# Attention rounds written out in place of a loop of two rounds, on all five engines of one Trainium2 core

## What is computed

```
x = x + attention(layernorm(x))             # 16 heads of 32, causal, softmax, output projection
x = x + xattn(ctx, ctx, layernorm(x))       # a long convolution of products k*v with a kernel per head, by q
x = x + ffn(layernorm(x))                   # weights and activations rounded to 8 bit, silu(gate) * up, down
```

## Time and profile before

| | us |
|---|---|
| median of 3 runs | 1241.2 (1239.53 to 1241.73) |
| the profiled execution | 1243.32 |
| its span, first to last instruction | 1241.5 |
| start of round 2 to end of round 13 (the loop) | 429.10 |

### The profile page before, as it was taken

How to read it: one execution, slowest core, us unless ns; L and a number is a source line. 1 busy time by engine, 2 the same in 40 slices (tenths; PEclk the granted TensorE clock), 3 DMA queues, 4 the chain that set the end, 5 groups by cost and what they waited for, 6 DMA issues and landing times. The chain is left out here.

```text
span 1241.5 us, 33761 instructions
## 1 busy us (share of the span) xinstructions
PE 1142.1 (92%) x10142; PEld 815.6 (66%) x10142; DVE 1006.6 (81%) x3165; ACT 880.2 (71%) x1815; POOL 963.1 (78%) x1112
## 2 busy tenths in 40 slices
PE   7989999999999999998756799999999999999996
PEld 5767777777777777875435566666666666666652
DVE  4678878878788887887486798888988988988885
ACT  3678888878788887888564366766667666667665
POOL 1286887767777776787833999999999999999993
PEclk8979999999999999999775999999999999999999
DMA  6346755556555555655382444434444333444310
GB/s 206 93 154 193 235 167 171 183 173 190 178 176 171 159 185 166 189 163 182 143 287 70 128 136 142 128 109 131 137 144 140 123 112 129 142 144 132 112 62 26
DMA packets 87840, 186.57 MB, mean 150 GB/s; under 512 B 12176, under 2 KB 28816, under 8 KB 87760
## 3 DMA queue, kind: packets, MB, share of 16 engines
q1 hardware_dynamic: 86896, 185.02, 47.2%
q10 hardware_dynamic: 864, 0.66, 0.3%
HBM read 105.86 MB, written 54.61 MB: 129 GB/s over the span
## 5 line engine op out<-in xcount | busy, mean ns | idle before, releaser
L649 ACT ACTIVATE prob<-masked,negmax 128x128 f32<-128x128 f32 (+1 forms) x512 | 206.4, 454 | 67.6 <-DVE negmax L777 66.6
L777 DVE CUSTOM_DVE_ANT_0 masked<-s_ps,mask_f 128x128 f32<-128x128 f32 (+1 forms) x512 | 161.1, 352 | 34.0 <-PE s_ps L530 21.5
L1028 PE MATMUL y_ps<-kv,toep 128*128 128x288 f16 x640 | 184.2, 288 | 1.4 <-DVE prod L1390 1.4
L1029 PE MATMUL y_ps<-kv,toep 128*128 128x288 f16 x640 | 183.8, 287 | 0.0
L1030 PE MATMUL y_ps<-kv,toep 128*128 128x288 f16 x640 | 183.8, 287 | 0.0
L1086 PE MATMUL f_ps<-w1T,xiT 128*128 128x512 bf16 (+1 forms) x768 | 172.9, 361 | 0.9 <-ACT xiT L1222 0.7
L1286 POOL TENSOR_TENSOR tree<-prod 128x512 f32<-128x512 f32 x128 | 163.3, 1276 | 1.3 <-DVE prod L1390 1.3
L1229 ACT ACTIVATE silu<-gate,sx 128x512 f32<-128x512 f32 (+1 forms) x96 | 66.0, 687 | 134.4 <-DVE gate L1454 134.3
L409 POOL TENSOR_TENSOR kv_s<-kv_f,kv_s 128x1152 f16<-128x1152 f32 x64 | 152.2, 2379 | 0.6 <-ACT kv_s L663 0.6
L783 DVE TENSOR_TENSOR pT_lo<-t_ps,pT_hi 128x384 f16<-128x384 f32 x256 | 140.7, 550 | 12.2 <-ACT pT_hi L657 11.7
L657 ACT CAST pT_hi<-t_ps 128x384 f16<-128x384 f32 x256 | 122.4, 479 | 34.4 <-PE t_ps L539 33.1
(11 more groups left out here) (162 smaller groups left out, 3505.6 us busy)
## 6 DMA issues: line engine op xcount, KB each, us to landing
kv_pairs<-kv_s SPq DMA_DIRECT2D x64, 576.0 KB, 3.3
kv<-kv_pairs SPq DMA_DIRECT2D x32, 1152.0 KB, 8.1
c_in<-in_ctxr SPq DMA_DIRECT2D x64, 192.0 KB, 2.5
x_in<-in_x SPq DMA_DIRECT2D x16, 512.0 KB, 6.4
q_st<-q_hi SPq DMA_DIRECT2D x128, 64.0 KB, 2.0
k_st<-k_hi SPq DMA_DIRECT2D x128, 64.0 KB, 2.0
x_res<-in_x SPq DMA_DIRECT2D x16, 512.0 KB, 5.9
x_after_attention<-x_out SPq DMA_DIRECT2D x16, 512.0 KB, 4.3
```

Of the source, the lines that this page charges most:

```text
L649: ins = nc.scalar.activation(prob[h % 2][:, at:at + w], masked[h % 2][:, at:at + w], ACT.Exp, bias=negmax[:, h % 2, t:t + 1], scale=-1.0)
L777: ins = nc.vector.tensor_tensor_reduce(masked[h % 2][:, at:at + w], s_ps[h % 2][:, at:at + w], mask_f[:, S - w:S], -1.0, FAR, ALU.add, ALU ...
L1028: nc.tensor.matmul(dst, toep[p][:, 0, taps], c[:, 0, m], start=mt == 0, stop=False)
L1029: nc.tensor.matmul(dst, toep[p][:, 0, taps], c[:, 1, m], start=False, stop=False)
```

## The change

On all five engines the hardware loop becomes a loop of the program that writes the kernel, so the twelve rounds 2 to 13 are written out one behind the other. In them i is now a number: waits compare with constants, DMA addresses are constants, and the register instructions, the branches, `alone`'s waits for register values and `lower_val` fall away where they depended on i being a register. `body` itself and every operation, buffer and order in it stay as they are.

```diff
@@ block.sync
-            with sp.Fori(LOOP0, LOOP1 - 1, 2) as i:
+            for i in range(LOOP0, LOOP1, 2):
                 body(i, 0)
                 body(i + 1, 1)
             for i in range(LOOP1, B):
@@ block.gpsimd
-            with pool.Fori(LOOP0, LOOP1 - 1, 2) as i:
+            for i in range(LOOP0, LOOP1, 2):
@@ block.tensor
-            with pe.Fori(LOOP0, LOOP1 - 1, 2) as i:
+            for i in range(LOOP0, LOOP1, 2):
@@ block.scalar
-            with act.Fori(LOOP0, LOOP1 - 1, 2) as i:
+            for i in range(LOOP0, LOOP1, 2):
@@ block.vector
-            with dve.Fori(LOOP0, LOOP1 - 1, 2) as i:
+            for i in range(LOOP0, LOOP1, 2):
```

## The result

The changed kernel takes 1234.1 us (median of 6 runs, 1232.27 to 1237.45) beside 1241.64 us for the kernel before (6 runs): a ratio of 0.9942 with a 95% interval of 0.9927 to 0.9957, 7.5 us less where 10.1 were forecast. Five of the six runs lie in the range 1227.5 to 1235.5. Run again beside more runs of before it is 1232.44 to 1240.24, 0.9932 (0.9915 to 0.9950).

What follows compares the result with a forecast made beforehand. PE was taken as the bound, nearly never idle in the attention loop and delayed by DVE refetching code at back edges. Savings of 8.0 + 2.1 = 10.1 us take 1241.2 to 1231.1 us, range 1227.5 to 1235.5.

Steps and rivals of the forecast that it cites:

- Term (a): Attention loop's five taken back edges: each costs PE 1.60 us, so 8.0 us saved; bounds nothing to 11 us.
- Term (b): Rounds 2 to 13, PE's wait at L468: constants replacing DVE's register arithmetic save 2.1 us; bounds 0 to 4.4.
- The 0.19 us at L468: PE's wait for DVE's aT_lo in written-out round 1, expected in all twelve rounds after the change.
- six even rounds gain 0.27 each: PE's wait at L468 in even rounds falls from 0.46 to 0.19 us through constants, 1.6 us in all.
- Term (c): Instruction fetch for the written-out rounds: more code is streamed ahead of its use on every engine, cost 0.
- Rival 3: Written-out rounds: straight code starves a sequencer; 50 packets at 1.60 us each cost 80 us, less 10; chance 0.03.
- Term (d): Rounds 0, 1, 14, 15 and everything after: same instructions, unchanged times; mixer's loop keeps 408.44 us for 12 passes.
- 1: Attention loop: only control is saved, slow even rounds come from something that stays; gain 0.9 us, to 1240.3; chance 0.04.
- 2: Attention loop: PE's wait at L468 and DVE's idle at back edges come in full; 15.4 us, to 1225.8; chance 0.05.
- 4: Mixer's loop: its code moves and DVE's body no longer stays, 1.6 us or more a pass; +9, 1250; chance 0.02.

Runs made afterwards that it cites:

- dve_only: Kernel before with only DVE's rounds written out, the loops of PE, ACT, POOL and SP kept: 1232.81 us, ratio 0.9941.
- dve_loop: Kernel before with the rounds of all engines but DVE written out, DVE keeping its loop: 1239.82 us, ratio 1.0001.
- pad66: Kernel before, all loops kept, with 66 small memsets in front of DVE's first work, shifting its loop: 1232.98 us, ratio 0.9944.
- pad112: Kernel before, all loops kept, with 112 small memsets in front of DVE's first work: 1238.32 us, ratio 0.9981.
- tail_before: Kernel before with idle matmuls (results unused) where PE waits in the last 40 us: 1239.73 us, ratio 1.0002.
- act_pad80: Kernel before, all loops kept, with 80 one-column copies in front of ACT's first small work, shifting ACT's loop: 1253.47 us, ratio 1.0094.
- after_pad64: Changed kernel with 64 small memsets in front of DVE's work, shifting its code: 1232.41 us.

## Why the prediction was right, and which terms were off

**The mechanism.** DVE's back edge is the gain: shown from both sides by dve_only and dve_loop, and its cause, code that is fetched again because of where the loop lies on blocks, by pad66 and pad112.

**Term (a), back edges, 8.0 us: too small by 0.9.** Rounds 3 to 13 sum to 393.91 us before and to 385.00 in pad66, whose loop stays: 8.9 us, 1.8 for each of the five even rounds, where the working had 1.60. The price of the branch itself was right: in pad112 round 2 takes 35.01 us and the five rounds behind a back edge 36.58 on the mean, 1.57 more. What was wrong is the step that took round 2, at 35.19 us, as a round in which DVE's code costs nothing. In pad66 the even rounds from 4 on take 35.01. The missing 0.2 us is a seam: the 32nd instruction of the loop's body, at place 97 + 31 = 128, is the first of a block. Timelines of DVE in round 2, first before, then pad112, where this instruction lies within a block:

```profile
118.73 0.49 DVE L794 TENSOR_TENSOR att<-o_ps,rsum 128x128 f32<-128x128 f32 x2
119.33 0.29 DVE L777 CUSTOM_DVE_ANT_0 masked<-s_ps,mask_f 128x128 f32<-128x128 f32 x1
```
```profile
117.15 0.49 DVE L795 TENSOR_TENSOR att<-o_ps,rsum 128x128 f32<-128x128 f32 x2
117.55 0.28 DVE L778 CUSTOM_DVE_ANT_0 masked<-s_ps,mask_f 128x128 f32<-128x128 f32 x1
```

The maxima start 0.60 us behind the division before, 0.40 in pad112. The delay of 0.2 us stands in all six passes of before, dve_loop, tail_before and act_pad80, where the loop lies the same, and in none of pad66 and pad112. So each even round of the old loop carried it, and the change took it away with the branches.

Round 2 of the changed kernel, 35.43 us, is slow for another reason. SP's 2 MB of w1 stand in the queue ahead of the rounds' transfers there, DMA engines are busy for 0.75 of it, and ACT waits for the store of kv_pairs:

```profile
ACT kv_s L663 <- DMA kv_pairs<-kv_s: 1.1, 1, 1.1
```

In the five profiles with DVE written out this wait and the round go together: 0.2, 0.7, 0.8, 1.1 and 1.4 us of it with 34.92, 35.01, 35.11, 35.43 and 35.64 us. It is not what made round 2 of the kernel before slow: that round takes 35.19 us in tail_before and 35.21 in act_pad80 too, where ACT doesn't wait for this store at all. Over the twelve profiles round 2 takes 34.92 to 36.05 us.

**Term (b), constants, 2.1 us: too large.** The 0.19 us at L468 came true (0.17 to 0.23, rounds 2 and 8 aside), but the step "six even rounds gain 0.27 each" failed: their 0.46 to 0.49 us was not register arithmetic. With the loop and without stall or seam in even rounds, in pad66, rounds 4 to 12 wait 0.28 us there. The rest was the seam in round 2 and the back edge in the others (0.47 to 0.50 in pad112 as well). Written out against shifted loop, rounds 3 to 13 sum to 384.46 and 385.00: 0.54 us, or 0.9 with round 8's seam of 0.35 put aside. That is the 0.08 us a round that the odd rounds had shown. Forecast and measured for the loop are 10.1 and 9.2 us (8.9 and 0.5, less 0.2 for the slower round 2); two errors of opposite sign made the sum better than its terms, which is luck.

**Term (c), fetching, 0: nearly.** The twelve rounds moved 37 packets of PE's queue and 29 of the others', and of rounds 3 to 13 only round 8 shows it, with 0.35 us. Not every seam of DVE costs: in round 10 one falls behind a wait as well, at 393.96, and the round takes 34.92 us. Rival 3's 1.6 us a packet is far off.

**Term (d), before and behind unchanged: wrong by about 2 us.** This is the part of the working that failed by its own sign: it said that it would be wrong if the stretch from round 14 to the end weren't the same within 1 us, and that stretch is 704.87 us in the profile after and 700.23 before, 4.6 more. Work and order are the same, and so is most of it: from round 14 to the first convolution 132.2 and 132.3 us, the mixer 533.1 in both. The tail is not: 34.94 before, 39.48 and 36.54 in two profiles of the changed kernel, 37.58 in dve_only. The granted clock fell there, and filling PE's idle time gives 3.0 us back in the changed kernel, by the medians, and nothing in the one before. What stays open is when the clock falls. Written-out rounds alone don't decide it: act_pad80 has all its loops and a tail of 36.54 us, after_pad64 has the rounds written out and a tail of 34.94, and the tails of pad66, pad112 and dve_loop held as well. With one profile a kernel this may be chance; the medians (7.5 and 7.8 us against 10.3 with fillers) speak for a tail that dips more often in the changed kernel, but nothing here shows it directly or gives a reason.

**Rivals.** 1 fell (even rounds behind a former back edge are 34.91 to 34.95 us, and 35.27 with round 8's seam), 2 had the sign of term (a)'s error but not its size, 3 fell as said. 4 did not come about, but its mechanism is real: pad66 and act_pad80 show that code put in front of a loop turns its stall off or on.

## What to carry to other kernels

When passes of a loop cost more than their rounds do written out, look at the sequencer's records behind the branch and at the instruction queue: silence of 3 us and packets in the middle of a loop mean that the loop doesn't stay. Here only the engine with the silence had to be written out, and a few dozen instructions in front of its loop did nearly as well; any edit ahead of a loop can bring the stall back. And a stretch that is taken as the undisturbed case, as round 2 was, should be compared with the same stretch of another kernel before its time is subtracted.

## What the runs showed of the hardware that was not expected

- What fits all runs is that DVE keeps four blocks of 128 instructions, the one fetched ahead among them: its body of 331 on three blocks stayed (5 packets, all in the first pass), on four it was fetched again, 31 packets in six passes and five in each later one. ACT's 276 instructions behaved likewise (26 packets more), if they lie as assumed. PE's body, on a queue of its own, moved six packets in the twelve rounds of every kernel that had its loop.
- A taken branch to code that had gone was followed by 2.8 to 3.3 us of silence on DVE and 2.5 to 3.2 on ACT, against 0.26 to 0.35 where the code had stayed. Of DVE's silence 1.6 us reached PE.
- A seam between blocks stopped DVE for 0.40 us in a row of small memsets and delayed the maxima in the old loop by 0.2 us in each pass. A written-out round lost 0.35 us to one where nothing hid it.
